# Grouping the row terms and the next image's projections of two strip pairs into every second step of a spectral layer

## The reference

```python
x = x + _L0_conv_ref(_gn(x), w_real, w_imag, b_real, b_imag)   # rfft2, complex 3x3 convolution of the spectrum, bias, irfft2
x = x + _L1_conv_ref(_gn(x))                                   # per-channel gates from row and column sums
x = x + _L2_conv_ref(_gn(x), W)                                # 3x3 convolution
x = x + _L3_conv_ref(_gn(x), weight)                           # 3x3 convolution
```

## Time and profile before

| | us |
|---|---|
| three runs | 4846.31, 4855.79, 4857.66 |
| median | 4855.79 |
| the profiled execution | 4858.67 |
| its span, first to last instruction | 4856.9 |
| granted TensorE clock, mean | 0.965 |

### The profile page before, as it was taken

How to read it: one execution, slowest core, us unless ns; L and a number is a source line. 1 busy time by engine, 2 the same in 40 slices (tenths; PEclk the granted TensorE clock), 3 DMA queues, 4 the chain that set the end, 5 groups by cost and what they waited for, 6 DMA issues and landing times.

```text
span 4856.9 us, 222294 instructions
## 1 busy us (share of the span) xinstructions
PE 4578.8 (94%) x84784; PEld 2919.9 (60%) x84784; DVE 2924.3 (60%) x10604; ACT 2482.2 (51%) x7085; POOL 3.2 (0%) x14
## 2 busy tenths in 40 slices
PE   5999999999999999999999999999999999988898
PEld 1555765556655666556655566555665556655566
DVE  2677717776277762777537774377734777257770
ACT  4555455544555445554455544555445554544435
POOL 0000000000000000000000000000000000000000
PEclk8999999999999999999999999999999999999999
DMA  6443036420364113541145411464014540233104
GB/s 193 114 123 93 6 80 177 141 74 17 93 176 138 54 26 105 174 129 44 32 113 167 129 36 36 116 178 124 24 40 132 168 119 19 51 112 106 54 4 142
DMA packets 290071, 468.15 MB, mean 96 GB/s; under 512 B 25393, under 2 KB 92145, under 8 KB 289265
## 3 DMA queue, kind: packets, MB, share of 16 engines
q1 hardware_dynamic: 289392, 458.29, 33.5%
HBM read 323.98 MB, written 134.22 MB: 94 GB/s over the span
## 4 chain that ended last, share of the span: by engine, by line
PE 92%; issue 3%; DVE 3%; ACT 1%; SPq 1%; ACTq 0%; DVEq 0%; DMA 0%
PE ps L1248 35%; PE ps L1168 19%; PE ps L1153 18%; PE ps L1161 6%; PE ps L1177 5%; PE ps L1027 5%; PE ps L1273 1%; PE ps L1073 1%; PE ps L1074 0%; PE ps L1100 0%; PE ps L1222 0%; PE ps L1300 0%; PE ps L1115 0%; ACT shared L491 0%; ACT x L566 0%
## 5 line engine op out<-in xcount | busy, mean ns | idle before, releaser
L1248 PE MATMUL ps<-x,conv_s 32*32 32x512 f32 x49104 | 1716.2, 602 | 21.9 <-issue 21.9
L1248 PEld LDWEIGHTS ps<-x,conv_s 32*32 32x32 f32 x49104 | 1229.5, 103 | 476.6 <-issue 234.6
L566 ACT ACTIVATE x<-ps,vec 128x256 f32 (+1 forms) x1024 | 490.6, 494 | 1017.9 <-PE ps L1168 1017.9
L817 DVE COPY vsb<-ps 128x512 f32<-128x512 f32 x512 | 329.7, 685 | 1128.3 <-PE ps L1153 1128.3
L1168 PE MATMUL ps<-hil,shared 128*128 128x256 f32 x4096 | 994.7, 386 | 0.0
L1168 PEld LDWEIGHTS ps<-hil,shared 128*128 128x128 f32 x4096 | 741.3, 191 | 274.6 <-issue 194.6
L805 DVE SCALAR_TENSOR_TENSOR shared<-xin,trig 128x256 f32<-128x256 f32 x2048 | 821.7, 440 | 57.5
L632 ACT ACTIVATE x<-ps,vec 64x512 f32<-64x512 f32 (+1 forms) x768 | 525.5, 684 | 424.7 <-PE ps L1248 414.4
L1153 PE MATMUL ps<-shared 32*32 32x512 f32 x16384 | 669.0, 614 | 3.8 <-issue 3.8
L623 ACT ACTIVATE x<-ps,vec 128x512 f32 x512 | 347.2, 684 | 467.9 <-PE ps L1248 467.9
L1153 PEld LDWEIGHTS ps<-shared 32*32 32x32 f32 x16384 | 309.0, 104 | 295.0 <-issue 231.8
(11 more groups left out here) (170 smaller groups left out, 2713.2 us busy)
## 6 DMA issues: line engine op xcount, KB each, us to landing
xin<-x SPq DMA_DIRECT2D x512, 256.0 KB
out<-x SPq DMA_DIRECT2D x512, 256.0 KB
shared<-x SPq DMA_DIRECT2D x448, 256.0 KB, 4.1
shared<-t_strip SPq DMA_DIRECT2D x512, 96.0 KB, 3.6
x<-x SPq DMA_DIRECT2D x64, 256.0 KB, 5.2
x<-t_proj SPq DMA_DIRECT2D x1, 2048.0 KB, 10.7
hil<-t_hil SPq DMA_DIRECT2D x1, 560.0 KB, 11.0
trig<-t_trig SPq DMA_DIRECT2D x1, 512.0 KB, 11.0
```

Source lines behind the costliest of these rows:

```text
L566: ins = nc.scalar.activation(split_in(strip_of(s))[:, q, :], split_in(ps[:, bank, :])[:, q, :], ACT.Identity, bias=v1(MEAN), accum_out=sum ...
L817: V.tensor_copy(vsb[:, e, :], ps[:, BV + e, :]).then_inc(v_copied, 1)
L1248: mm = pe.matmul(ps[TM * cg:TM * cg + TM, banks[k], :], conv_s[TM * rg:TM * rg + TM, kw, second, :], x1[TM * rg:TM * rg + TM, of, kw:kw + ...
```

## The change

The two groups that are neither mixing nor Hilbert product are taken out of even steps. In an odd step `add_u` is called for pair t-1 and then for pair t, whose mixing has just been done, and at its end `project_next` for pair t-1 and then for pair t. The even step has mixing, Hilbert products and transpositions alone. The call of `add_u` and the call of `project_next` for the last pair, which stood behind the last step, go, since step 31 is odd. The number of matmuls stays; no other engine's program is changed.

```diff
                     mix(t, odd)
-                    add_u(t - 1, 1 - odd, table, table_uses)
+                    if odd:
+                        for pair in range(2):
+                            add_u(t - 1 + pair, pair, table + 2 * pair, table_uses)
                     for e in range(2):
                         hilbert(t * 2 - 2 + e, e, 1 - odd)
                         turn(t * 2 + e, e)
-                    project_next(2 * (1 - odd), table, uses, first)
+                    if odd:
+                        for pair in range(2):
+                            project_next(2 * pair, table + 2 * pair, uses, first and pair == 0)
...
-                add_u(PAIRS - 1, 1, TABLES - 2, STRIPS // TABLES - 1)
                 for e in range(2):
                     hilbert(STRIPS - 2 + e, e, 1)
...
                 mm.then_inc(e_done, 1)
-                project_next(2, TABLES - 2, PAIRS // 2 - 1, False)
```

## The result

The changed kernel takes 5440.66 us, median of five runs (5434.10 to 5458.78), against 4854.20 for the kernel before. The ratio is 1.122, 95% interval 1.1197 to 1.1242. The profiled execution has a span of 5432.0 us, 575.1 more than before. The forecast was 5485, range 5370 to 5600.

What follows compares the result with a forecast made beforehand. It took each step as a chain from mixing to eviction, with loads late for moved projections: 4856.9 + 192 (quiet) + 322 (stores) + 7 (step 31) + 77 + 31 (clock) = 5486 span, forecast 5485 us, range 5370 to 5600.

Steps and rivals of the forecast that it cites:

- What bounds the step: Each step is a chain from mixing to eviction; row terms (1.06 us) are on it, projections hide behind the eviction.
- The lateness: Odd steps 1 to 29, images 0 to 6: next-image loads land too late for projections; 105 stalls, some 430 us; 83%.
- The landing: Second next-image load in odd steps: lands 6.06 us after the first Hilbert product, 9.4 in steps with stores.
- what the stores add: Two stores ahead of the loads in 48 odd steps: stall near 5.9 us, +6.70 a pair against +3.36 quiet.
- The second groups: Odd steps: a second group of row terms and of projections, each 0.96 us, with 0.1 either way for row terms.
- (c): Rival: SP is further ahead, loads not late; the second projection group costs its own time, +0.86 a pair, 4953 us; 6%.
- 7 us for step 31: Step 31, no load stall: second row-term group stands ahead of the last four Hilbert products, +0.9 us eight times.
- The clock: TensorE at 1.2 GHz after stalls: 1.6 us for each of 48 with stores (77), 0.55 for each of 57 quiet (31).
- One in three: Quiet stalls of 2.5 us: one in three followed by the low clock at 1.63 us, 0.55 each, 31 us in all.
- (b): Rival: every one of the 105 stalls drops the clock and costs its upper end, 2.6 or 1.63 us; about 5595 us; 8%.
- (d): Rival: TensorE alone sets the pace and each change of matmul shape costs it; faster, -37 us, 4819 us; 3%.

Runs made afterwards that it cites:

- first run: Changed kernel with the next image's loads of pair q+1 moved in SP's queue ahead of the tables of pair q+3; 5147.72 us, ratio 1.0618.

## Why the prediction was right

**What bounds the step.** Held in both halves. The row terms were on the chain: grouped alone they move the time, and the even step without them and without projections is 9.01 us (1088.64 to 1097.65), forecast 9.02. The projections were in the shadow of the eviction: taken out of the even step they leave TensorE waiting 1.0 us for L566, and nothing is gained.

**The lateness.** Held: 105 waits, 57 short and 48 long, in the place and of the cause named; 386.7 us for a forecast of some 430. The quiet stalls are 2.23 us on average beside about 2.5, those with stores 5.41 beside 5.9. The landing was sized a little long: second loads land 5.86 us after the first Hilbert product where I had taken 6.06, and with stores 9.05 for 9.4. That the stores' landings would come earlier than before, once the next strips' loads are out of their way, held: 9.05 us on average for 9.48 in the kernel before. The run with the loads first takes all waits away and 527 of the 586 us with them (5440.66 to 4913.66). The part of the argument that said what the stores add held as well: moving the loads ahead of them gave back 180 us.

**The second groups.** Mis-sized: 0.96 us each was taken, 0.86 was measured for row terms and for projections. The estimate from Hilbert records counted their modelled ends, so it came out at 0.95 (1.89 us with the end, but 1.73 from the group's start to that of the next group, and half of that is 0.86); the bound of 0.1 below it was where the value lay. It is a part of why rival (c), worked out as 4953, came out as 4914 when it was made true: two groups, 0.1 less each, are 21 of these 39 us. The 7 us for step 31 did not show either, and the rest was not taken apart. It is also why the row terms alone are a gain.

**The clock.** The term for stalls with stores was 1.6 us a pair, 77 us; filling the stall gave 1.85 a pair, 89 us. It was too small, and the term for the landing too large, so the sum for these pairs, 8.30, lies close to the measured 8.03; that the two errors partly cancel is luck. For the quiet ones 3.91 was forecast and 3.52 measured. There the clock's term was nearly met and the other terms were too long. The granted clock fell to 0.50 behind 17 of the 57 quiet stalls, and these pairs take 24.93 us for 23.23 of the other 40, 0.2 of it a longer stall. Spread over all 57 that is about 0.45 for a term of 0.55. One in three had been a choice, with no row of such a short pause behind it, so this too is luck. One of the 17, image 2 (TensorE, and the window: length, TensorE busy, granted clock, DMA share, GB/s):

```profile
1742.06 1.97 PE L1027 MATMUL ps<-shared 128*64 128x512 f32 x4 [2.57 <-DMA shared<-x]
...
1742.00:1745.40 3.40, 3.34 (x36) 0.51 0.00 0
```

The differences between forecast and measured pairs make 35 of the 54 us by which the sum was too long (629 for 575). The rest lies outside the pairs: 7 us were added there for step 31, and that part of the images is 11 us shorter.

**Rivals.** (b), every stall paying its upper end, did not happen: in the second half of image 2's stage, with seven quiet stalls, the mean clock is 0.98, and two of the seven were followed by 0.50:

```profile
1681.98:1848.30 166.32, 142.91 (x1796) 0.98 0.39 108
```

In all, the long stalls paid 48 times of 48 and the short ones 17 times of 57. The Trainium skill, page "TensorE: Matmul & The Clock Gate", section "HAM oscillation — how this bites in real kernels", tells of a kernel that fell to the low clock after every wait for a DMA, and puts those waits at about 3 to 5 us. The long stalls here (4.96 to 6.04 us) agree with it; the prediction stretched it to the short ones (1.54 to 2.61 us), which are below the waits that it tells of. (c), loads in time, is not this kernel but a neighbour of it. (d), TensorE alone setting the pace, fell with the 1.01 us waits for L566 in the run where no load is late. Its idea that a change of shape costs time did hold, 0.2 us for a group, and it is the whole gain of the row terms' grouping.

## What to carry to other kernels

Before a consumer is moved forward, follow its input back through the queue that issues it: here the load left behind a wait on the very step that was to use it, and no change in the consumer's program shows that. A TensorE share of 94% does not mean that work on TensorE costs its length; the projections were free where they stood, in the shadow of an eviction, and cost 0.86 us each time where they were put. Split such an edit in its halves: one was worth 0.4%, the other cost 13%. Do not size an effect by one step: the one shown of the first run waits 0.94 us, and its mean is 1.65.

## What the runs showed of the hardware

A four-record group of two float32 matmuls of 512 columns that run side by side costs 1.06 us between other shapes and 0.86 behind another of its kind (64-row tiles); with 64-column tiles it is 1.01 and 0.86.

The landing of a 256 KB load depends much on what was issued just ahead of it in the same queue. Medians for the second load of an odd step: 3.6 us behind two table loads of 96 KB (changed kernel, quiet steps), 4.6 with two stores between (its steps with stores), 5.9 behind two loads of its own size (first run), 3.7 with no other load just ahead (loads first, quiet steps).

Useless work can pay: 48 times 4.56 us of extra matmuls inside waits made the kernel 103 us faster, as TensorE came out of the waits at 2.4 instead of 1.2 GHz.

Short waits can cost the clock too, and their length does not settle it. Of the 57 quiet stalls, with TensorE busy on both sides, 17 were followed by 1.2 GHz: those were 1.80 to 2.61 us long, the other 40 were 1.54 to 2.53.
